# Causal attention: the value product of two heads in float16 parts, and inputs of two later stages held on the chip

## The reference

```python
x = x + _L0_attn_ref(_L0_cond_ref(cond, cond, x, coupling, bias), Wqkv_w, Wqkv_b)
x = x + _L0_ffn_ref(_L0_cond2_ref(x, cond, ada_w, ada_b, qkv_w, qkv_b, ...), ...)

def _L0_attn_ref(x, Wqkv_w, Wqkv_b):        # 16 heads of 32
    q, k, v = ...                            # q, k rotated
    scores = jnp.einsum('bthd,bshd->bhts', q, k * scale)
    scores = scores + causal_mask
    attn = jax.nn.softmax(scores, axis=-1)
    out = jnp.einsum('bhts,bshd->bthd', attn, v)

def _L0_cond2_ref(x, timestep_embed, ...):   # 16 heads of 128
    x1 = _ln(x) * (1.0 + scale1) + shift1
    ...                                      # full softmax attention
    x = x + gate1 * attn_out
    x2 = _ln(x) * (1.0 + scale2) + shift2
    h = jax.nn.gelu(x2 @ ffn_w1 + ffn_b1, approximate=False)
    x = x + gate2 * (h @ ffn_w2 + ffn_b2)
```

## Time and profile before

| | before |
|---|---|
| median of 3 runs | 5189.52 us (5189.28 to 5210.45) |
| profiled execution | 5189.95 us |
| its span, first to last instruction | 5188.1 us |
| mean granted TensorE clock | 0.709 |
| busy: PE / PEld / DVE / ACT / POOL | 4557.2 / 3811.5 / 4040.3 / 2368.0 / 1673.5 us |

### The profile page before, as it was taken

The page is one execution under the profiler, slowest core; times in us unless marked ns, Lnnn a source line. Parts: engine busy times, 40 slices in busy tenths (PEclk is TensorE's granted clock), DMA queues, the critical chain, the costliest instruction groups (busy, mean ns, idle before and its releaser), DMA issues. The chain is left out here.

```text
span 5188.1 us, 213435 instructions
## 1 busy us (share of the span) xinstructions
PE 4557.2 (88%) x78597; PEld 3811.5 (73%) x78597; DVE 4040.3 (78%) x25233; ACT 2368.0 (46%) x11552; POOL 1673.5 (32%) x5950
## 2 busy tenths in 40 slices
PE   6998878878888788788888897999999999699899
PEld 5896666666666666666666796787777887578787
DVE  7999999999999999999999465777777777521123
ACT  4444444444444444444444564655555455332243
POOL 2444444444444444444444341233233232100000
PEclk5555555555555555555555898999999999799999
DMA  3000010000000000001000332122222222130211
GB/s 114 20 22 2 1 36 1 2 22 1 22 2 1 22 1 2 22 1 23 2 1 22 111 107 85 55 78 82 94 74 78 80 72 78 52 123 33 87 61 41
DMA packets 229212, 224.43 MB, mean 43 GB/s; under 512 B 82108, under 2 KB 152452, under 8 KB 228488
## 3 DMA queue, kind: packets, MB, share of 16 engines
q1 hardware_dynamic: 225216, 216.64, 13.4%
q10 hardware_dynamic: 3208, 0.68, 0.1%
q0 software_dynamic: 192, 0.03, 0.0%
HBM read 160.50 MB, written 56.80 MB: 42 GB/s over the span
## 5 line engine op out<-in xcount | busy, mean ns | idle before, releaser
L457 PEld LDWEIGHTS bank<-tanh_parts,w_lo 128*128 128x128 f16 x32768 | 1040.9, 105 | 795.6 <-ACT tanh_parts L296 794.4
L457 PE MATMUL bank<-tanh_parts,w_lo 128*128 128x4 f16 x32768 | 1210.1, 169 | 417.1 <-ACT tanh_parts L296 304.2
L296 ACT ACTIVATE tanh_parts<-ys 128x8 f16<-128x8 f32 x4096 | 857.5, 209 | 1572.5 <-DVE ys L592 1571.3
L465 PE MATMUL bank<-tanh_parts,w_hi 128*128 128x8 f16 x32768 | 1174.2, 173 | 3.9 <-issue 3.9
L465 PEld LDWEIGHTS bank<-tanh_parts,w_hi 128*128 128x128 f16 x32768 | 1033.2, 104 | 4.0 <-issue 4.0
L592 DVE TENSOR_TENSOR_SCAN ys<-mix,bank 128x24 f32<-128x24 f32 x4096 | 822.0, 203 | 78.8 <-PE bank L465 6.8
L297 ACT ACTIVATE tanh_full<-ys 128x8 f32<-128x8 f32 x4096 | 804.6, 196 | 0.0
L582 DVE TENSOR_TENSOR tanh_parts<-tanh_full,tanh_parts 128x8 f16<-128x8 f32 x4096 | 646.9, 164 | 2.6 <-ACT tanh_full L297 1.0
L1358 POOL TENSOR_TENSOR t_w_qk<-t_raw_qk,t_w_qk 128x512 fp32r<-128x512 f32 x128 | 168.2, 1336 | 686.6 <-ACT t_w_qk L1522 686.6
L777 PE MATMUL t_bank<-t_x,t_w_qk 128*128 128x512 f32 x1536 | 361.5, 391 | 12.8 <-DVE t_x L1778 12.8
L777 PEld LDWEIGHTS t_bank<-t_x,t_w_qk 128*128 128x128 f32 x1536 | 290.2, 189 | 74.0 <-DVE t_x L1778 13.5
(11 more groups left out here) (203 smaller groups left out, 9240.5 us busy)
## 6 DMA issues: line engine op xcount, KB each, us to landing
t_raw_qk<-L_cond_qkv_w_dram SPq DMA_DIRECT2D x128, 256.0 KB, 3.2
t_raw_vo<-L_cond_qkv_w_dram SPq DMA_DIRECT2D x16, 1024.0 KB, 5.1
t_raw_vo<-L_cond_out_w_dram SPq DMA_DIRECT2D x16, 1024.0 KB, 5.2
n<-t_parts SPq DMA_DIRECT2D x14, 1024.0 KB, 6.6
u_t<-u_out SPq DMA_DIRECT2D x32, 256.0 KB, 2.7
u<-u_t SPq DMA_DIRECT2D x32, 256.0 KB, 2.8
swapped<-swapped_t SPq DMA_DIRECT2D x32, 256.0 KB, 3.0
g_raw<-L_cond_ffn_w_dram SPq DMA_DIRECT2D x8, 1024.0 KB, 10.1
```

The lines of the kernel that those rows point to most:

```text
L296: act.activation(tanh_parts[:, u, at, :, 0], ys[:, s, at, :, 2], ACT.Tanh, scale=1.0 / SCALE).then_inc(s_th, 1)
L457: pe.matmul(sums[:, :, 2], w_lo[:, w_of, k, m * P:(m + 1) * P], tanh_parts[:, u, k, :, 0], start=(m % 2 == 0 and k == 0), stop=False, skip ...
L465: last = pe.matmul(sums[:, :, 1:3], w_hi[:, w_of, k, m * P:(m + 1) * P], tanh_parts[:, u, k], start=False, stop=(m % 2 == 1 and k == C - 1 ...
```

## The change

**Causal values.** In each round, heads 0 and 1 get three float16 products for each block in place of one fp32 product. ScalarE writes the transposed probabilities times 8192 as a float16 high part (`high`), and VectorE computes the low part from the PSUM bank and the high part (`low`); that instruction now frees the bank. `low` of head 0 stands between the maxima of heads 1 and 2 of the next round, `low` of head 1 between those of heads 2 and 3. Heads 2 and 3 stay fp32, and both copies are ScalarE's; VectorE has no copy left. The values v of heads 0 and 1 are split into parts once for each row and tile (`values_high` on ScalarE, `values_low` on VectorE, 16 times each).

**Early inputs.** The second attention's identity, bias rows, ada table, first weights and the gelu layer's biases are loaded during the scan into buffers that stay allocated; row 0 of x is loaded once the causal phase has stored it. The gelu layer takes row 3 first, from the SBUF buffers in which the attention leaves it, so its normed parts and its base are neither stored nor loaded; its first two weight tiles are issued before the attention's end, into buffers whose last use by the attention is over.

```diff
                     sp.wait_ge(s_ada_done, ADA)
-                    sp.dma_start(ada_dram, ada[:, :, :]).then_inc(s_out, 16)
+                    sp.dma_start(held["bias_rows"][0:48, :], io["L0_cond2_qkv_b"].rearrange("(m p) -> m p", p=P)).then_inc(s_held, 16)
...
+                    for x in range(2):
+                        sp.dma_start(held["raw_qk"][:, x], qkv_w[:, :, x * INNER:x * INNER + DH1]).then_inc(s_held, 16)
+                    sp.dma_start(held["raw_vo"], qkv_w[:, :, 2 * INNER:2 * INNER + 512]).then_inc(s_held, 16)
...
-ACT_HEADS = 3
+
+
+FAST, PT_SCALE, V_SCALE, VALUES_AHEAD = 2, 8192.0, 64.0, 1
...
+def value_at(k):
+
+    row, tile = (k + VALUES_AHEAD) // 12, (k + VALUES_AHEAD) % 12
+    return (row, tile) if tile < TT and 0 <= row < B else None
...
-            if head[0] != "row" and head[1] < ACT_HEADS:
+            if head[0] != "row" and head[1] >= FAST:
...
+                if row == 0:
+                    sp.dma_start(held["src"], xa_dram[:, :, 0, :]).then_inc(s_src, 16)
+            sp.wait_ge(s_src, 16)
...
+                    pe.wait_ge(s_vlo, row * TT + ROUND_TILES[k % 3][-1] + 1)
                 blocks = ROUND_BLOCKS[k % 3]
                 for x, (i, s) in enumerate(blocks):
                     low, high = out_columns(k, j, i)
-                    last = pe.matmul(out_bank[:, low:high], pt[:, k % 2, j, x * P:(x + 1) * P], val[:, row % 2, s, h],
-                                     start=(j == 0 and x == 0), stop=(j == 3 and x == len(blocks) - 1), skip_group_check=True)
+                    of = slice(x * P, (x + 1) * P)
+                    if j < FAST:
+                        for a, b in PRODUCTS:
+                            pe.matmul(out_bank[:, low:high], pt_parts[a][:, k % 2, j, of], val_parts[b][:, row % 2, s, h // 4, j],
+                                      start=(j == 0 and x == 0 and a + b == 0), stop=False, skip_group_check=True)
+                    else:
+                        last = pe.matmul(out_bank[:, low:high], pt[:, k % 2, j - FAST, of], val[:, row % 2, s, h],
+                                         start=False, stop=(j == 3 and x == len(blocks) - 1), skip_group_check=True)
...
+                if j == FAST and k >= 2:
+                    act.wait_ge(s_valued, k - 1)
+                act.activation(pt[:, k % 2, j - FAST, 0:width(k)], turn_bank[use_of[k, j] % 2][:, 0:width(k)], ACT.Copy).then_inc(s_freed_act, 1)
+
+            def high(k, j):
+                act.wait_ge(s_turned, use_of[k, j] + 1)
                 if j == 0 and k >= 2:
                     act.wait_ge(s_valued, k - 1)
-                act.activation(pt[:, k % 2, j, 0:width(k)], turn_bank[use_of[k, j] % 2][:, 0:width(k)], ACT.Copy).then_inc(s_freed_act, 1)
+                act.activation(pt_parts[0][:, k % 2, j, 0:width(k)], turn_bank[use_of[k, j] % 2][:, 0:width(k)], ACT.Copy,
+                               scale=PT_SCALE).then_inc(s_high, 1)
+
+            def values_high(row, tile):
+                act.wait_ge(s_v[row % 2], 16 * (row // 2 + 1))
+                if row >= 2:
+                    act.wait_ge(s_valued, 12 * (row - 1))
+                of = val[:, row % 2, tile].rearrange("p (g j) n -> p g j n", j=4)
+                act.activation(val_parts[0][:, row % 2, tile], of[:, :, 0:FAST, :], ACT.Copy, scale=V_SCALE).then_inc(s_vhi, 1)
 
             for k in range(-AHEAD, ROUNDS + 3):
-                older = tile_at(k - 1)
+                value, older = value_at(k), tile_at(k - 1)
                 if older:
                     rotated_high(older)
+                if value:
+                    values_high(*value)
                 for j in range(4):
                     if 0 <= k < ROUNDS:
                         exps(k, j)
-                    if 0 <= k - 1 < ROUNDS and j < ACT_HEADS:
-                        copied(k - 1, j)
+                    if 0 <= k - 1 < ROUNDS:
+                        (high if j < FAST else copied)(k - 1, j)
...
-                v.wait_ge(s_turned, use_of[k, j] + 1)
-                if k >= 2:
-                    v.wait_ge(s_valued, k - 1)
-                v.tensor_copy(pt[:, k % 2, j, 0:width(k)], turn_bank[use_of[k, j] % 2][:, 0:width(k)]).then_inc(s_freed_dve, 1)
+            def low(k, j):
+                v.wait_ge(s_high, FAST * k + j + 1)
+                v.scalar_tensor_tensor(out=pt_parts[1][:, k % 2, j, 0:width(k)], in0=turn_bank[use_of[k, j] % 2][:, 0:width(k)], scalar=PT_SCALE,
+                                       in1=pt_parts[0][:, k % 2, j, 0:width(k)], op0=ALU.mult, op1=ALU.subtract).then_inc(s_freed_dve, 1)
+
+            def values_low(row, tile):
+                v.wait_ge(s_vhi, row * TT + tile + 1)
+                of = val[:, row % 2, tile].rearrange("p (g j) n -> p g j n", j=4)
+                v.scalar_tensor_tensor(out=val_parts[1][:, row % 2, tile], in0=of[:, :, 0:FAST, :], scalar=V_SCALE,
+                                       in1=val_parts[0][:, row % 2, tile], op0=ALU.mult, op1=ALU.subtract).then_inc(s_vlo, 1)
...
-                now = tile_at(k)
+                now, value = tile_at(k), value_at(k)
                 for j in range(4):
                     if 0 <= k < ROUNDS:
                         peaks(k, j)
                     if j == 1 and now:
                         rotate_second(now)
-                if 0 <= k - 1 < ROUNDS:
-                    for j in range(ACT_HEADS, 4):
-                        copied(k - 1, j)
+                    if j == 1 and value:
+                        values_low(*value)
+                    if 1 <= j <= FAST and 0 <= k - 1 < ROUNDS:
+                        low(k - 1, j - 1)
...
-            load_src(0)
-            sp.dma_start(identity[:, :], io["const_identity"]).then_inc(s_ident, 16)
-            load_qk(0)
-            load_vo(0)
...
-            store_norm(LAST)
-            store_base(LAST)
-            sp.wait_ge(s_nout, 32 * LAST)
-            sp.wait_ge(s_nbase, 16 * B)
+
+            sp.wait_ge(s_volo, len(plan.weights))
+            sp.dma_start(raw_vo, gelu_load(io, 0)).then_inc(s_next, 16)
+            sp.wait_ge(s_turned, 4 * HEADS)
+            sp.dma_start(probs, gelu_load(io, 1)).then_inc(s_next, 16)
+            sp.wait_ge(s_next, 32)
+            sp.wait_ge(s_nout, 32 * (LAST - 1))
+            sp.wait_ge(s_nbase, 16 * (B - 1))
...
+        ROWS = (0, 1, 2, 3) if sign else (3, 0, 1, 2)
+        HELD_LOADS = 0 if sign else 2
...
-            load(0)
-            load_x(0)
-            load(1)
+            if sign:
+                load(0)
+                load_x(0)
+                load(1)
             load(2)
-            sp.dma_start(base[:, :, :], row_of(base_dram, 0)).then_inc(s_base, 16)
+            if sign:
+                sp.dma_start(base, row_of(base_dram, ROWS[0])).then_inc(s_base, 16)
```

195 lines of the change are left out of this document (98 added, 97 removed).

## The result

The changed kernel takes 5209.06 us (median of 20 runs, 5202.20 to 5223.62) against 5189.44 (20 runs); the ratio is 1.0027 with a 95% interval of 1.0016 to 1.0037. It is slower by about 0.3%. The medians lie 0.38% apart, because 15 of the 20 runs of the kernel before took 5186 to 5200 us and the other five 5207 to 5213.

| from ... to | before | after | difference |
|---|---|---|---|
| start to the first causal mask | 2886.99 | 2890.58 | +3.6 |
| first causal mask to the first mask of round 48 | 279.7 | 323.4 | +43.7 |
| from there to the attention's opening | 26.6 | 24.3 | −2.3 |
| its opening to the norm's first step | 6.9 | 0.0 | −6.9 |
| from there to the end of the last norm | 1320.2 | 1317.6 | −2.6 |

The account below looks back on a forecast made before the run. Scores, maxima and exponentials were taken to bound causal rounds A and C, TensorE round B. Chain +22, clock +18 and phase starts −24.5 gave +15 on the profiled 5189.95: 5204 us, range 5146 to 5255.

Parts of the forecast that it names:

- Who bounds the rounds: Causal stage: scores, maxima, exponentials and next mask bound rounds A and C; TensorE, 98% busy, bounds only round B.
- Round C +0.70: Causal round C, low parts 384 wide: the last exponential starts 3.53 us after the first instead of 2.83.
- round A +0.56: Causal round A, low parts 512 wide: the last exponential starts 3.83 us after the first, before 3.26; +0.56 taken.
- Round B −0.07: Causal round B: next masks at 4.01 us after the first exponential instead of 4.08, head 2's transposes released at about 1.66.
- Chain +22: Causal stage: three rounds cost 1.2 us, sixteen times +19; low parts of v +2, turns between rows +1.
- Float16 products: TensorE, causal rounds: 0.05 us per product; round B's 24 last 1.3 us, before low part 0 frees the bank: no cost.
- Clock +18: Causal stage: TensorE's busy share falls to 78 to 87%, so part of the stage runs at half clock, +18 us.
- R1: Rival: TensorE's clock stays full in the causal stage, as there is no long pause; 5187 us, chance 0.22.
- price of half clock: Causal stage: half clock adds 6.9 us to a period of three rounds, +110 us if all sixteen periods run so.
- in a few places only: Profile after: the causal windows' granted clock lies below 1.00 in a few places only.
- one sixth of the stage at half: Causal stage: share at half clock, chosen between 0 and 110 us, giving +18 us.
- Starts −24.5: Phase starts: the second attention's wait for row 0 goes, −6.9 us; the first gelu product comes earlier, −17.6 us.

Follow-up runs that it names:

- Narrow low parts: The changed kernel with each low part of the probabilities computed for 16 columns only, the rest left zero; 5161.37 us.
- filler kernel: The changed kernel with 16 more products of mask and identity, into an unread PSUM bank, behind the float16 values of heads 0 and 1; 5181.35 us.
- one fast head: The changed kernel with one head in float16 parts instead of two; 5209.38 us.
- reordered fp32: The changed kernel with all values in fp32, three banks for transposes, ScalarE's exponentials 1 and 2 earlier, values of heads 2 and 3 before head 3's transposes; 5184.87 us.
- starts only: The changed kernel with the causal stage's values whole in fp32 again, as before, keeping the early inputs; 5165.21 us.

## Why the prediction was right

The forecast was 5204 us, +14, and 5209 came: +15 in the profiled execution, +0.27% (14 us) by ratio, +20 between the medians. The chances gave this case 0.45. Its steps:

- **Who bounds the rounds.** Right: exponentials of A and C, with TensorE at 98% as a misleading number. Narrow low parts bring A and C back to their old lengths.
- **Round C +0.70, round A +0.56.** Measured +0.53 (6.02 against 5.49) and +0.32 (6.29 against 5.97), in the filler kernel, whose clock is full. Low parts last 0.55 and 0.69 us and the next instruction starts 0.48 and 0.61 after their start, where 0.61 and 0.75 were taken in full: here the recorded length of an instruction on VectorE reaches past the start of the next, and the row of line 1099 has the length, not the distance. The sum was also loose: with its own lengths low part 1 would end at 2.95 and 3.33, not 2.9 and 3.24, and the two terms would be about 0.78 and 0.66.
- **Round B −0.07.** Wrong in sign, +0.14 (5.96 against 5.82). The transposes of head 2 start 1.88 us behind the first exponential (2957.02), not 1.66, since the rotation ahead of the low part takes 0.92 there (0.68 before; why is open). The 2.35 us behind them were right.
- **Chain +22.** Measured 17.4 with the clock held by the filler.
- **Float16 products.** 0.05 us was taken, 0.025 measured. It is hidden by the wait for the low part either way. The Trainium skill's 81 ns for a stream of weight load and product pairs ("TensorE: Matmul & The Clock Gate", section "Back-to-back issue gap"), weighed there against this change, is stated for 128 columns. The prediction carried it over to products with 33, and for these it doesn't hold in the trace: eighteen pairs started within 0.42 us.
- **Clock +18.** Measured 26. The term was needed and R1 (clock stays) is out: without it the time would have been near the filler's. The price of half clock was right: 6.9 us on a period of 18.3, so 6.9 of 25.2 us at half, gives an estimate of 26 for the 95 us that the trace has at half. The share was not: 26 of 110 is 24% of the work, not one sixth, and "in a few places only" were fourteen. The step "one sixth of the stage at half", argued from the busy share, was a choice between two distant rows; that it came as near as this is luck. And its reason is incomplete: the clock also fell with TensorE busy without a gap, and with one fast head at a higher share. The Trainium skill (same page, section "HAM oscillation — how this bites in real kernels") ties the fall to long idle gaps; here it fell with no wait above 1.4 us in the changed kernel and with none in the 13 us before the first fall in the reordered fp32 one, so the traces don't agree with that rule.
- **Starts −24.5.** Measured −6.9 and −17.8, and −24 for the kernel with the starts only. The share of 7.3 for the wait, 2.6 for the issues and about 1 for the barrier was right.

Of the two errors, 5 us too much for the chain and 8 too little for the clock, one paid for the other, which is luck; the small terms not forecast (+3.6 in the scan, −2.6 and −2.5 in the attention and the gelu layers) cancel as well, and single executions of either kernel differ by more.

## What to carry to other kernels

An engine that is busy 98% of a stage need not bound it: look whether the same short wait ends on the same other engine in each round. Where it does, relief for the busy engine buys nothing until the chain is shortened, and an instruction put into the chain costs what it waits for and what it lasts together, less what stood to spare at that place. So work out the spare time of each place in the order before choosing one. Where the clock of TensorE depends on what it does, less work for it can cost more than the work did; hold the clock with filler once, to learn how much of a difference is the clock's.

## What was not expected of the hardware

- The clock fell from 1.00 to 0.50 in a stretch that TensorE spent without a gap (3.40 of 3.40 us busy, 10.30 of 10.30 before it), and stayed when the same value products stood in another order (mean 0.98 against 0.83 in 276 us, one trace each). What it goes by stays open; these runs only exclude the busy share and idle gaps as the whole answer.
- In the reordered fp32 kernel rounds last 10 to 11 us at half clock and stretches of up to 37.5 us stay there, and runs of this kernel spread over 55 us, where those of the kernel before spread over 27 beside it.
- Sixteen additional products in each of 48 rounds made the kernel 28 us faster.
- Float16 products with 33 moving columns and a weight load for each start 0.025 us apart.
- On VectorE the next instruction starts 0.48 us after a low part of 384 columns that is recorded with 0.55, and 0.61 after one of 512 recorded with 0.69.
